# Three output-state matmuls and a 24-row group change places in a Mamba block kernel

## The reference

```python
proj = jnp.einsum('bsd,ed->bse', x, in_proj_w)          # gate, x, B, C, dt
...
A_cum = jnp.cumsum(A_dt, axis=-1)
L = jnp.exp(_segsum(A_dt))                              # decays inside a chunk
Y_diag = jnp.einsum('bzlhn,bzshn,bhzls,bzshp->bzlhp', Cc, Bc, L, xch)
...
prev = new_states[:, :-1]                               # state before each chunk
Y_off = jnp.einsum('bzlhn,bzhpn,bhzl->bzlhp', Cc, prev, jnp.exp(A_cum))
Y = (Y_diag + Y_off).reshape(b, s, H, P) + hs * D[None, None, :, None]
g = y * jax.nn.silu(gate)
```

## Time and profile before

| | |
|---|---|
| three runs, median | 1795.99 us (1793.48 to 1796.66) |
| profiled execution, its own time | 1795.91 us |
| its span | 1794.1 us |
| TensorE busy | 97% of the span |
| VectorE, ScalarE, GpSimd busy | 77%, 60%, 54% |
| mean granted TensorE clock | 0.989 |

### The profile page before, as it was taken

The page is one execution under the profiler, slowest core; times in us unless marked ns, Lnnn a source line. Parts: engine busy times, 40 slices in busy tenths (PEclk is TensorE's granted clock), DMA queues, the critical chain, the costliest instruction groups (busy, mean ns, idle before and its releaser), DMA issues.

```text
span 1794.1 us, 31771 instructions
## 1 busy us (share of the span) xinstructions
PE 1732.6 (97%) x9818; PEld 1356.3 (76%) x9818; DVE 1378.8 (77%) x2266; ACT 1078.3 (60%) x1830; POOL 977.6 (54%) x732
## 2 busy tenths in 40 slices
PE   6899999999999999999999999999999999999988
PEld 4677778777777777777777777777777777877766
DVE  4777788777877788877887778777888778876776
ACT  6566565666646665665656666566665656466644
POOL 1545465655536475454646555365754556676651
PEclk9899999999999999999999999999999999999999
DMA  6312121111212121121211112121211212221111
GB/s 230 114 33 68 59 71 45 50 62 49 74 34 68 51 72 53 32 68 61 69 47 50 57 55 74 34 68 51 72 53 27 73 57 74 79 62 59 52 48 59
DMA packets 80936, 112.97 MB, mean 63 GB/s; under 512 B 28402, under 2 KB 32498, under 8 KB 79988
## 3 DMA queue, kind: packets, MB, share of 16 engines
q1 hardware_dynamic: 62898, 78.24, 14.9%
q10 hardware_dynamic: 17858, 32.52, 5.4%
HBM read 88.42 MB, written 22.29 MB: 62 GB/s over the span
## 4 chain that ended last, share of the span: by engine, by line
issue 46%; POOL 36%; PE 10%; DVE 3%; ACT 3%; POOLq 1%; DMA 0%; SPq 0%; ACTq 0%; DVEq 0%
POOL yt L1801 10%; POOL ssq L1796 7%; POOL prev L1778 6%; POOL wg_lo L1704 4%; POOL wo_lo L1704 3%; POOL yt L1804 3%; POOL wx_lo L1704 3%; PE bank L506 2%; PE bank L507 2%; PE bank L508 2%; PE bank L897 1%; PE bank L767 1%; DMA gate<-w_mod_dram 0%; PE bank L542 0%; POOL acc L1724 0%
## 5 line engine op out<-in xcount | busy, mean ns | idle before, releaser
L1801 POOL TENSOR_TENSOR yt<-yt,ea 128x384 f32<-128x384 f32 (+1 forms) x128 | 189.6, 1481 | 377.5 <-DVE ea L1612 377.5
L1582 DVE TENSOR_TENSOR lm<-lm,cbm 128x512 f32<-128x512 f32 x256 | 189.5, 781 | 147.8 <-ACT lm L1181 147.0
L1377 DVE SCALAR_TENSOR_TENSOR xc<-bank,bpar,xc 128x511 f32<-128x511 f32 (+2 forms) x384 | 285.6, 744 | 6.8
L506 PE MATMUL bank<-h_hi,wg_hi 128*128 128x512 f32 x640 | 261.9, 409 | 18.2 <-ACT gate L1106 8.0
L508 PE MATMUL bank<-h_hi,wg_lo 128*128 128x512 f32 x640 | 250.8, 392 | 0.0
L507 PE MATMUL bank<-h_lo,wg_hi 128*128 128x512 f32 x640 | 250.4, 391 | 0.0
L1778 POOL TENSOR_TENSOR prev<-prev,dec 128x512 f32<-128x512 f32 x96 | 129.8, 1352 | 156.5 <-DVE prev L1523 91.3
L506 PE MATMUL bank<-h_hi,wx_hi 128*128 128x512 f32 x512 | 211.0, 412 | 3.3 <-DVE bt L1377 2.2
L506 PE MATMUL bank<-wo_hi,g_hi 128*128 128x512 f32 x496 | 206.3, 416 | 0.0
L508 PE MATMUL bank<-h_hi,wx_lo 128*128 128x512 f32 x512 | 200.8, 392 | 0.0
L507 PE MATMUL bank<-h_lo,wx_hi 128*128 128x512 f32 x512 | 199.9, 390 | 0.0
(11 more groups left out here) (222 smaller groups left out, 3935.1 us busy)
## 6 DMA issues: line engine op xcount, KB each, us to landing
raw_w<-w_in_dram SPq DMA_DIRECT2D x145, 256.0 KB, 2.6
raw_w<-w_out_dram SPq DMA_DIRECT2D x64, 256.0 KB, 2.6
part_d<-part ACTq DMA_DIRECT2D x64, 256.0 KB, 2.2
part<-part_d ACTq DMA_DIRECT2D x60, 256.0 KB, 2.8
rt<-rows_d SPq DMA_DIRECT2D x256, 6.0 KB
acc<-x_dram SPq DMA_DIRECT2D x8, 256.0 KB, 6.6
acc<-w_mod_dram SPq DMA_DIRECT2D x2, 1024.0 KB, 5.9
lh<-neg_d SPq DMA_DIRECT2D x128, 6.0 KB
```

The costliest lines, as they stand in the source:

```text
L506: nc.tensor.matmul(out_ap, whi(k), hhi(k), start=(k == 0), stop=False)
L1377: stt(dst[:, at], ps[:, 0:HALF - 3 + k], w(k), dst[:, at], ALU.mult, ALU.add)\
L1582: tt(lm[:, h % 4, :], lm[:, h % 4, :], cbm[:, toks(hf)], ALU.mult).then_inc(v_m, 1)
L1801: tt(yt[:, j % 2, cols], yt[:, j % 2, cols], ea[:, j % 2, cols], ALU.add).then_inc(p_t3, 1)
```

## The change

In the loop over a unit's tiles, the 24-row group for the next tile stood ahead of the tile's output-state products in tiles 0, 1 and 2. Now it does so in tile 0 alone. In tiles 1 and 2 it stands behind them and ahead of the masked products. Each instruction and each wait is the same as before; the lines below the edit have moved by 5 (L860 is now L865).

```diff
                 for j in range(NCT):
-                    if j < NCT - 1:
+                    if j == 0:
                         exp_a(j + 1)
                         diff(2 * j + 2)
                         diff(2 * j + 3)
...
                         lst = nc.tensor.matmul(bank[yo_bank(end, j)][:, chunk(z)], prev[:, slot(hf, z), j * 128:(j + 1) * 128],
                                                ct[:, toks(hf, z, 1)], start=True, stop=True)
                     lst.then_inc(t_yo, 1)
+
+                    if 0 < j < NCT - 1:
+                        exp_a(j + 1)
+                        diff(2 * j + 2)
+                        diff(2 * j + 3)
 
                     te.wait_ge(v_m, 8 * u + 2 * j + 2)
```

## The result

The changed kernel took 1821.81 us (median of 4 runs, 1821.50 to 1822.43), against 1795.65 for the kernel before beside it (4 runs): a ratio of 1.0146, 95% interval 1.0131 to 1.0161. It is 26 us slower. The prediction was 1820 us, slower with a chance of 0.88.

A forecast was written before the change was run, and what follows sets the result against it. Though TensorE is busy 1732.6 of 1794.1 us, a slackless chain through ScalarE, VectorE and GpSimd was taken to set each unit's end. Delays of 10.7, 7.1 and 6.2 us sum to 24.0: 1820 us, range 1807 to 1827.

The forecast's parts named there:

- The array's own time: TensorE's row in tiles 1 and 2: one shape switch less, 1.32 us instead of 1.51, 0.19 less per tile.
- the rival in which the array's saving carries: 62 tiles at 0.19 us give 11.8 us less, 1784 us; chance 0.08.
- The circuit: ScalarE, VectorE, GpSimd beside TensorE: tile 1's 24-row group, and the whole chain, 0.67 us later, 0.89 for odd c.
- The wait before L843 of tile 2: TensorE waits some 0.8 us for VectorE's L1612 of tile 1, in 24 units, some 19 us in all.
- A small step that was off: Tile 2: L843 behind the wait takes 0.76 us to the 24-row group; masked products start 0.42 us late.
- The end of the unit: At the next unit's gate the late chain decides: units 0.67 us longer for c = 0 and 2, 0.89 otherwise.
- the sum: All units together: 10.7 us for c = 0 and 2, 7.1 for c = 1, 6.2 for c = 3; 24.0 us.
- The rival that counted TensorE's lateness alone: Only TensorE's lateness is paid: 13.9 us, 1810 us; chance 0.15, shared with anything between it and the forecast.
- Units with c = 3: L843 of tile 3 starts 0.55 us late, waiting some 0.9 us; unit costs 0.55 to 0.89, upper taken.
- The last unit: No projections between its tiles and TensorE waits for ScalarE anyway: 0 us added.

The follow-up runs named there:

- tile 2 alone: Kernel before, with the new order (output-state products, then the 24-row group) in tile 2 only: 1796.96 us against 1796.28, ratio 1.0001.
- the short mask: VectorE's mask of tile 2's second head cut from 512 to 64 columns, all units but last: 1806.46 us on the kernel after, 1781.04 on the kernel before.
- the group moved the other way: Kernel before, with tile 1's 24-row group moved ahead of the second projection behind tile 0, all units but the last: 1778.53 us, ratio 0.9903.
- tile 1 alone: Kernel before, with the new order in tile 1 only, tile 2 keeping the old: 1819.98 us, ratio 1.0127.

## Why the prediction was right

*The array's own time.* Forecast 0.19 us less in a tile, with the step from the 24-row group to 64-column products taken at 0.33. Measured 753.74 - 752.42 = 1.32 to the masked products, the step itself 0.33. Right, and worth nothing in time, as tile 2 alone showed. With that the rival in which the array's saving carries (1784) is out.

*The circuit.* Forecast 0.67 and 0.89 us; counted from the last projection the copy came 0.67 us later for c = 0 and 2 and 0.89 for c = 1 and 3, in each of the 31 units. Right, and shown as the cause by the two experiments with one tile each, by the short mask, which takes time out of the chain alone, and by the group moved the other way.

*The wait before L843 of tile 2.* Forecast some 0.8 us; in the profile 0.66 idle after the modelled end, and 758.43 - 757.38 = 1.05 where 0.23 is usual: 0.82. Idle time in the 24 units sums to 16.7 us, where the forecast had some 19. The group of tile 2 started 1.92 us after the last projection (757.38 to 759.30), where it was 0.32 before and 1.03 with tile 2 alone. That cost nothing: with tile 1 alone this group stands ahead of the wait again, and the time is the same.

*A small step that was off.* L843 behind the wait took 0.87 us to the group and not 0.76 (758.43 to 759.30), so the masked products of tile 2 were 0.52 us late and not 0.42. Nothing hung on it.

*The end of the unit.* Forecast 0.67, 0.89, 0.67 and 0.89 out of 0.55 to 0.89; measured 0.65, 0.88, 0.69, 0.83: 23.7 us where the sum had 24.0. The rival that counted TensorE's lateness alone (13.9 us) is out: that sum is 10 us short.

*Units with c = 3.* TensorE's wait before L843 of tile 3, forecast from 0.39 us of room and 0.89 of delay:

```profile
919.58 0.68 DVE L1617 TENSOR_TENSOR ea<-bank,ea 128x512 f32<-128x512 f32 x1
...
920.31 1.16 PE L843 MATMUL bank<-ct,prev 128*128 128x128 f32 x8 [0.75 <-DVE ea L1617]
```

The wait was forecast at some 0.9 us; the trace counts 0.75 idle behind the modelled end. L843 starts 0.56 us later than before, counted from tile 0's masked products, on average (forecast 0.55).

*The last unit.* This is the term that was wrong: forecast 0; the unit's last sum comes 1.05 us later. I had seen that TensorE waits for ScalarE there, and not that with no projections between, moving the group behind L843 delays ScalarE's decays and GpSimd in turn just the same. With it the sum is 25 us, and 26 were measured. That they come so close is in part luck, since the tail's clock adds and takes away as much as the term itself.

## What to carry to other kernels

Before matmuls are reordered to save array time, follow each group to the engine that consumes it: if that engine is idle until it comes, the group's place in the row is worth more than the switches. A share of 97% for one engine doesn't say that it is the bound; look at what ended its few short waits, and follow that chain back to where it last leaves the busy engine's own row. A group there is worth issuing early until its consumer is held by something else: here moving one group gave 1% (1778.5 us), and moving the second as well gave nothing that is clear of noise (1776.0).

## What the runs showed of the hardware

A wait of TensorE can shrink without any effect on the time: its waits before L843 fell from 22.1 us in the kernel after to 13.0 with tile 1 alone, at 1822 and 1820 us, which can't be told apart. The size of such a wait is no measure of its cost.

A step into or out of the 24-row shape next to 512-column matmuls cost 0.09 to 0.10 us at the step: 0.32 instead of 0.23 from a projection to the 24-row group, and 0.31 to 0.33 instead of 0.23 from it to the 128-column products, to the 64-column products or back to projections. From a projection to the 128-column products there is no such cost (0.23). The first group of products behind a 24-row group or behind a wait takes 0.10 us more than behind a projection: 0.86 or 0.87 against 0.76, and 1.09 against 0.98 for four. With the new order in tile 2 alone, the three products behind a projection took 0.80 us, between the two.

At the lower level of the granted clock (0.50) the 48 filler matmuls of the tail took 10.09 us from first to last, at the full level 5.30. Which of the two a run of this kernel gets there differs from trace to trace, and it moves the end by more than the term of the last unit does.
